# Expert and shared biases of a mixture-of-experts layer: from dense gates and a matmul to adding gathers and GpSimd

## The reference

```
k, v = xn @ key_w.T, xn @ value_w.T ; r = sigmoid(xn @ recep_w.T)
out  = x + (r * wkv_scan(decay, first, k, v)) @ out_w.T          # attention-like mixing over time
logits = xn @ gate_w.T + gate_b ; top 2 of 8 experts, weights g  # routing
y  = sum over the 2 chosen e of g_e * ((silu(xn@w1_e.T+b1_e) * (xn@w3_e.T+b3_e)) @ w2_e.T + b2_e)
z  = (silu(xn@ws1.T+bs1) * (xn@ws3.T+bs3)) @ ws2.T + bs2         # shared expert, 512 wide
out += y + z
```

## Time and profile before

| | |
|---|---|
| time, median of 3 runs | 473.65 us (469.54 to 474.90) |
| the profiled execution | 470.54 us, of which the span of the records is 468.8 us |
| PE busy | 445.1 us (95%) |
| DVE busy | 365.1 us (78%) |
| ACT busy | 239.8 us (51%) |
| POOL busy | 232.5 us (50%) |
| mean granted clock of PE | 0.981 |

### The profile page before, as it was taken

The page is one execution under the profiler, slowest core; times in us unless marked ns, Lnnn a source line. Parts: engine busy times, 40 slices in busy tenths (PEclk is TensorE's granted clock), DMA queues, the critical chain, the costliest instruction groups (busy, mean ns, idle before and its releaser), DMA issues.

```text
span 468.8 us, 8342 instructions
## 1 busy us (share of the span) xinstructions
PE 445.1 (95%) x2549; PEld 374.1 (80%) x2549; DVE 365.1 (78%) x680; ACT 239.8 (51%) x394; POOL 232.5 (50%) x224
## 2 busy tenths in 40 slices
PE   5898977979999999999998999999999999999997
PEld 4453746858888888888887879798888889898987
DVE  5968868798776987878675689996968687877863
ACT  4778735677768586876754532423324142324031
POOL 3234777354858658589744477661523425160000
PEclk9899769999999999999999999999999999999999
DMA  8999743255674854344454863726152433431001
GB/s 245 396 351 285 211 115 94 66 199 203 237 264 120 273 183 139 125 136 135 119 198 158 290 238 113 251 68 228 50 185 86 155 122 123 157 119 63 25 24 45
DMA packets 45874, 77.24 MB, mean 165 GB/s; under 512 B 5924, under 2 KB 32268, under 8 KB 45836
## 3 DMA queue, kind: packets, MB, share of 16 engines
q1 hardware_dynamic: 36924, 55.83, 33.8%
q0 software_dynamic: 8240, 20.88, 16.9%
q10 hardware_dynamic: 672, 0.04, 0.1%
HBM read 48.52 MB, written 28.21 MB: 164 GB/s over the span
## 4 chain that ended last, share of the span: by engine, by line
PE 46%; POOL 18%; issue 13%; DVE 10%; DMA 4%; ACT 4%; SPq 3%; POOLq 0%; DVEq 0%; ACTq 0%
POOL xg L1005 8%; PE ps_w L1540 5%; PE ps_w L1542 5%; PE ps_w L1541 5%; PE ps_w L1605 5%; PE ps_w L1606 5%; PE ps_w L1607 5%; PE ps_g L1082 4%; DMA w_lo<-w_all 3%; POOL den L1017 2%; PE ps_y L1082 2%; SPq L424 2%; POOL den L1016 2%; DVE stats L687 2%; POOL firsts L1024 2%
## 5 line engine op out<-in xcount | busy, mean ns | idle before, releaser
L1005 POOL DMA_INDIRECT xg<-xn_rows,tile_tok x71 | 71.4, 1006 | 21.9 <-issue 19.1
L1516 POOL DMA_INDIRECT yg<-expert_rows,rows x64 | 66.8, 1044 | 23.6 <-issue 17.1
L1082 PE MATMUL ps_g<-w_hi,x_hi 128*128 x142 | 56.7, 399 | 1.6 <-DVE x_lo L1237 1.6
L1082 PE MATMUL ps_g<-w_lo,x_hi 128*128 x142 | 56.7, 399 | 0.0
L1082 PE MATMUL ps_g<-w_hi,x_lo 128*128 x142 | 56.3, 397 | 0.0
L1647 ACT ACTIVATE sact<-ps_w,vec_b 128x512 f32<-128x512 f32 x32 | 22.0, 687 | 58.7 <-PE ps_w L1542 58.7
L1540 PE MATMUL ps_w<-col_hi,s_hi 128*128 128x512 f32 x128 | 50.5, 395 | 0.4 <-DVE shid L1758 0.4
L1542 PE MATMUL ps_w<-col_hi,s_lo 128*128 128x512 f32 x128 | 50.2, 392 | 0.0
L1541 PE MATMUL ps_w<-col_lo,s_hi 128*128 128x512 f32 x128 | 50.1, 392 | 0.0
L1082 PE MATMUL ps_y<-w_hi,h_hi 128*128 x142 | 43.1, 304 | 1.3 <-DVE h_lo L1253 1.3
L1246 DVE TENSOR_TENSOR hid<-ps_g,act 128x512 f32<-128x512 f32 (+1 forms) x36 | 23.7, 657 | 25.5 <-ACT act L1158 25.5
(11 more groups left out here) (247 smaller groups left out, 1278.5 us busy)
## 6 DMA issues: line engine op xcount, KB each, us to landing
expert_rows<-y SPq DMA_DIRECT2D x35, 256.0 KB, 2.2
w_lo<-w_all SPq DMA_DIRECT2D x16, 384.0 KB, 10.1
table<-mix_tables SPq DMA_DIRECT2D x8, 768.0 KB, 6.7
xT<-x SPq DMA_DIRECT2D x16, 256.0 KB, 6.1
xn_rows<-xn SPq DMA_DIRECT2D x16, 256.0 KB, 9.2
xn_columns<-xT SPq DMA_DIRECT2D x8, 512.0 KB
col<-xn_columns SPq DMA_DIRECT2D x8, 512.0 KB, 5.0
res<-x SPq DMA_DIRECT2D x16, 256.0 KB, 2.9
```

The costliest lines, as they stand in the source:

```text
L1005: pool.indirect_dma_start(out=xg[b][:, t, :], out_offset=None, in_=xn_d[:, :], in_offset=bass.IndirectOffsetOnAxis(ap=tile_tok[:, first_ti ...
L1082: mm = nc.tensor.matmul(out, x[:, k, :], w[:, ds(e, 1), k, cols].rearrange("p o n -> p (o n)"), start=(k == 0 and n == 0), stop=(last and ...
L1516: pool.indirect_dma_start(out=yg[a.buf(2)][:, k, q, :], out_offset=None, in_=y_d[:, :], in_offset=bass.IndirectOffsetOnAxis(ap=picked[a.bu ...
```

## The change

The bias terms leave the matmul. `b_all` becomes a table of 9 rows: `bs2`, then `b2` of the experts in falling order. In `choose` the rank of each chosen expert (8 minus its number) is kept in `rank` rather than overwritten, and clipped to 1..8 it is the row number of that expert's bias (`bias_row`, in one tile `picks` with `slots`). In the mixing stage GpSimd's gather of step a is followed by `add_biases`: once the 8 gathers have landed, 8 more indirect DMAs fetch the bias rows and add them onto `yg`; and by `add_shared`: one GpSimd addition of `bs2` onto `res`. `dense`, `terms`, `gT`, `g_now`, `rows_b`, `low_rows`, PE's 8 transposes and its 32 bias matmuls go, with their loads and waits. DVE's first 6 weight cuts (`split_lo`) stand together at the end of routing, where there were 2. DVE's first group of each step now waits for `b_bias` and `b_rows`.

```diff
-            nc.gpsimd.memset(terms[:], 0.0).then_inc(s_terms, 1)
-            pool.wait_ge(s_terms, 1)
-            nc.gpsimd.memset(terms[:, :, 3 * E:3 * E + 2], 1.0).then_inc(s_terms, 1)
...
-                own.link(nc.vector.tensor_reduce(red[:, t], work2[:, t], AX_X, ALU.max))
+                own.link(nc.vector.tensor_reduce(rank[:, 0, t], work2[:, t], AX_X, ALU.max))
...
-        MADE, BOTH, HIGH, LOW = 4, 6, 13, 2
+        MADE, BOTH, HIGH, LOW = 4, 6, 13, 6
...
-            own.link(nc.vector.tensor_copy(tile_exp[:], exp_f[:]))
-            scaled()
-            dve.wait_ge(s_terms, 2)
-            nc.vector.tensor_tensor(dense[:], score, mask[:].rearrange("p e j -> p j e"), ALU.mult).then_inc(s_terms, 1)
+            nc.vector.tensor_copy(tile_exp[:], exp_f[:]).then_inc(s_ready, 1)
+            own.link(nc.vector.reciprocal(gates[:, 0, :], red[:]))
             dve.wait_ge(s_gate, 1)
             nc.vector.tensor_tensor(gates[:, 1, :], gates[:, 1, :], gates[:, 0, :], ALU.mult)
-            dve.wait_ge(s_terms, 4)
-            nc.vector.tensor_tensor(terms[:, :, E:2 * E], dense[:], terms[:, :, 0:E], ALU.subtract
-                                    ).then_inc(s_terms, 1)
+            nc.vector.tensor_scalar(bias_row, rank[:], 1.0, float(E), ALU.max, ALU.min).then_inc(s_ready, 1)
...
-            pe.wait_ge(s_terms, 5)
-            for i in range(NSTEP):
-                mm = nc.tensor.transpose(ps_y[i // 4][:].rearrange("p t c -> p (t c)")[:, i % 4 * P:(i % 4 + 1) * P],
-                                         terms[:, i * Q:(i + 1) * Q, :].rearrange("p q n -> p (q n)"), ident[:])
-                if i % 4 == 3:
-                    mm.then_inc(c_turn, 1)
+            pe.wait_ge(s_ready, 1)
...
-            def pick(a):
-                at_least(pool, b_o, a.i * Q - Q)
-                nc.gpsimd.tensor_copy(g_now[a.buf(2)][:], gT[:, ds(a.i, 1), :].rearrange("p o n -> p (o n)")
-                                      ).then_inc(b_gc, 1)
+            def add_biases(a):
+                pool.wait_ge(b_gath[a.buf(2)], (a.uses(2) + 1) * 16 * TOPK * Q)
+                pool.sem_inc(b_go, 1)
+                for k in range(TOPK):
+                    for q in range(Q):
+                        pool.indirect_dma_start(
+                            out=yg[a.buf(2)][:, k, q, :], out_offset=None, in_=b_all,
+                            in_offset=bass.IndirectOffsetOnAxis(ap=picked[a.buf(2)][:, TOPK + k, q:q + 1], axis=0),
+                            compute_op=ALU.add
+                        ).then_inc(b_rows[a.buf(2)], 16)
+
+            def add_shared(a):
+                pool.wait_ge(b_res[a.buf(2)], (a.uses(2) + 1) * 32)
+                nc.gpsimd.tensor_tensor(res[a.buf(2)][:], res[a.buf(2)][:],
+                                        shared_b[:, None, :].broadcast_to([P, Q, C]), ALU.add).then_inc(b_bias, 1)
+
+            def prepare(a):
+                gather(a)
+                add_biases(a)
+                add_shared(a)
 
             def step(a, first, left):
-                pick(a)
                 if left > 0:
-                    gather(a.plus(1))
+                    prepare(a.plus(1))
...
-                    nc.tensor.matmul(ps_w[q][:, 0:C], g_now[a.buf(2)][:], rows_b[:, q, :],
-                                     start=True, stop=False)
                     for k in range(KC):
                         three_rows(ps_w[q][:, 0:C], a_hi, a_lo, k, slice(q * P, (q + 1) * P), o_hi, o_lo,
-                                   False, False)
+                                   k == 0, False)
...
                 if g == 0:
-                    dve.wait_ge(b_res[buf], (a.uses(2) + 1) * 32)
-                    dve.wait_ge(b_gath[buf], (a.uses(2) + 1) * 16 * TOPK * Q)
+                    dve.wait_ge(b_bias, a.i + 1)
+                    dve.wait_ge(b_rows[buf], (a.uses(2) + 1) * 16 * TOPK * Q)
...
-        "b_all": np.concatenate([get("L0_ffn_b2")] * 3 + [get("L0_ffn_bs2")[None]] * 2, axis=0),
+        "b_all": np.concatenate([get("L0_ffn_bs2")[None], get("L0_ffn_b2")[::-1]], axis=0),
```

More of the change, by code:

```diff
@@ L55 @@
 EPS = 1e-5
-TERMS = 32
 PIECE = 256
@@ L224, in _, with route @@
                 mix_vector(dve)
-def route(nc, kept, x, first, decay, vec_tf, vec_td, gate_w, gate_b, w_all, w_first, nw_d, xn_d, xT_d, ident, slots, gates,
-          tile_tok, tile_exp, w_hi, w_lo, terms, lane_i, row_of1, minus):
+def route(nc, kept, x, first, decay, vec_tf, vec_td, gate_w, gate_b, w_all, w_first, nw_d, xn_d, xT_d, ident, slots, bias_row, gates,
+          tile_tok, tile_exp, w_hi, w_lo, lane_i, row_of1, minus):
     with ExitStack() as ctx:
@@ L568, in scalar @@
                 split(i)
[L569 to L572, removed]
             for i in range(4, BOTH):
@@ L984, in sync @@
                     sp.dma_start(*loads[a - A_LOADS]).then_inc(c_ld, 16)
-                if a == A_ROWS:
-                    sp.wait_ge(c_zero, 1)
-                    for q in range(Q):
-                        sp.dma_start(rows[TERMS * q:TERMS * q + 3 * E + 2, q, :], b_all).then_inc(c_rows, 16)
                 if a == 4 * LAST_V + 1:
@@ L1194, in scalar @@
             cut_x(0)
-            for h in range(2):
-                act.wait_ge(c_turn, h + 1)
-                nc.scalar.activation(gT[:, 4 * h:4 * h + 4, :].rearrange("p j n -> p (j n)"),
-                                     ps_y[h][:].rearrange("p t c -> p (t c)"), ACT.Copy).then_inc(c_gT, 1)
             silu(0)
@@ L1217, in scalar @@
                     halves(v)
-                if a == A_HI:
-                    act.wait_ge(c_rows, 16 * Q)
-                    act.wait_ge(c_zero, 1)
-                    nc.scalar.activation(rows_hi[:], rows[:], ACT.Copy).then_inc(c_rhi, 1)
                 if a == DUOS - 4:
@@ L1365, in vector, with mix @@
                     differences(v + 1)
-                if a == A_ZERO + 2:
-                    low_mask()
-        return sync, gpsimd, tensor, scalar, vector, (c_y, c_yc, c_wlo, c_gT, c_rowsb)
-def mix(nc, kept, over, x, xT_d, y_d, y_stored, coef_stored, tab_d, out, slots, gates, vr_hi, vr_lo, raw_s13, raw_o, raw_s2,
-        col0, col_hi0, col_lo0, vec_b1, vec_b3, gT, rows_b):
+        return sync, gpsimd, tensor, scalar, vector, (c_y, c_yc, c_wlo, (c_ld, len(loads)), s_ready)
+def mix(nc, kept, over, x, xT_d, y_d, y_stored, coef_stored, tab_d, out, picks, b_all, shared_b, gates, vr_hi, vr_lo, raw_s13, raw_o,
+        raw_s2, xT, x_hi, x_lo, vec_b1, vec_b3):
     with ExitStack() as ctx:
@@ L1388, in mix @@
         splits = ((raw_s13, s13_hi, s13_lo), (raw_o, o_hi, o_lo), (raw_s2, s2_hi, s2_lo))
-        xT = [col0, sb("col1", [P, KC, STEP], F32)]
-        x_hi = [col_hi0, sb("col_hi1", [P, KC, STEP], F32R)]
-        x_lo = [col_lo0, sb("col_lo1", [P, KC, STEP], F32R)]
         res = [sb(f"res{b}", [P, Q, C], F32) for b in range(2)]
         yg = [sb(f"yg{b}", [P, TOPK, Q, C], F32) for b in range(2)]
-        picked = [sb(f"rows{b}", [P, TOPK, Q], I32) for b in range(2)]
+        picked = [sb(f"rows{b}", [P, 2 * TOPK, Q], I32) for b in range(2)]
         sa = sb("sa", [P, KC * B, TIMES + 1], F32)
-        g_now = [sb(f"g_now{b}", [P, P], F32R) for b in range(2)]
         table = [sb(f"table{b}", [P, 3, KC, TIMES], F32) for b in range(2)]
@@ L1424, in mix @@
         b_xlo = sem("b_xlo")
-        b_gc = sem("b_gc")
+        b_rows = [sem(f"b_rows{b}") for b in range(2)]
+        b_bias = sem("b_bias")
         b_v = sem("b_v")
```

95 lines of the change are left out of this document (27 added, 68 removed).

## The result

The changed kernel takes **545.12 us** (median of 4 runs, 543.77 to 545.86) against 471.6 us on the same chip: 1.155 times as long, 95% interval 1.146 to 1.164. The forecast was 512 us with a range up to 537. The direction and the mechanism came true; the time lies above the range. The profiled execution took 543.77 us, its span is 542.0.

What follows compares the result with a forecast made beforehand. GpSimd was taken to bound mixing: first `prepare` ends at 292.7, seven more at 28.7 us reach 493.6, plus 17 us tail and 1.7 us beyond the span give 512 us; range 494 to 531, widened to 490 to 537.

Steps and rivals of the forecast that it cites:

- the mechanism: Mixing stage: GpSimd becomes the bound at 26 to 31 us a step, where PE would need 25.0; chance 0.81.
- A: GpSimd's price for one adding gather of bias rows in `prepare`: taken as 1.24 us, between 0.95 and 1.53.
- The rule weighed beside it: GpSimd computes one descriptor pair per DMA operation regardless of bytes, so the whole 0.58 us would belong to the addition.
- signs of being wrong: GpSimd still waits for `b_slot`; median A outside 0.95 to 1.53 us; DVE waits for landing well after GpSimd's addition.
- The sum: GpSimd's work for one mixing step: 11.9 + 1.85 + 0.3 + 12.0 + 2.4 + 0.2 = 28.7 us.
- The upper end: Mixing stage: adding costs GpSimd all of the difference, A = 1.53 us, a step 31.0 us, the kernel 531 us.
- The second rival: Mixing stage: adding is dearer still, 1.79 us each as routing's mean, a step 33.1 us, 547 us; chance 0.11.
- The head: Start of mixing: second `prepare` ends at 321.4 where its rows were wanted at 298.90, most of the loss.
- The tail: From the last `prepare`, ending at 493.6, to the span's end: 17 us, against 18.7 before, PE having worked ahead.
- The gain taken off beforehand: Mixing stage: removing PE's 32 bias matmuls saves 3.8 us, 0.48 us a step, only while PE sets the pace.

Runs made afterwards that it cites:

- the run with three lengths: Changed kernel with each step's bias gathers replaced by six: rows of 1 KB, 512 B and 2 KB, each with and without addition; 508.40 us, one run.

## Why the prediction was wrong, point by point

- **Right: the mechanism.** GpSimd bounds the mixing stage, with no wait for DVE left in its loop; DVE stands at the first group of `experts`, and PE waits for `shid` behind it. Without the adding gathers the loss is zero, so they carry it. The addition of `bs2` costs something too, some 3.7 us by one pair of traces, which the products that went make up for in part.
- **The step that failed: "I take half for the addition, A = 1.24 us, because it is equally near to both rows."** It measured 1.54 us, and 1.70 in the mean. The half was no reading of the trace: two causes lay between two rows, and one of them was worth nothing. The rule weighed beside it gave all of the 0.58 us to the addition, and the run with three lengths bears it out (0.6 us, at every length).
- **Two of the prediction's own signs of being wrong came up.** The median of A is 1.540 us, just outside 0.95 to 1.53. And in four of the eight steps the landing of the added rows, not the addition of `bs2`, ends DVE's wait, 0.7 to 4.9 us after that addition is done. In the step shown above the addition ends at 422.20 + 2.93 = 425.13, and the use comes 4.9 us later:
```profile
430.03 0.88 DVE L1662 SCALAR_TENSOR_TENSOR res<-yg,gates,res 128x256 f32<-128x256 f32 x2 [11.30 <-DMA yg<-b_all,rows]
```
  The sum had no term for that landing (4.4 us in the median, up to 8.7). It moves single uses, but not the pace, since GpSimd goes on without waiting for them.
- **The upper end was no bound.** 531 us took 1.53, the least price of the earlier trace rows, although the mean of the earlier trace rows was 1.79. Above the least price lies what DVE does in SBUF beside it, 0.16 us in the mean, as the two kernels with added DVE work bear out. The second rival came nearest (547 us), but for its number only: it named weight loads, and I gave it 0.11. My range ended at 537.
- **The rest of the sum holds.** With 1.70 in place of 1.24 the eight gathers take 8 x 1.70 + 2.1 = 15.7 us. The first `prepare` then ends at 261.7 + 34.7 = 296.4 (measured: the use at 296.45), a step takes 32.4 us (measured 32.34), and the last use comes at 522.9 (measured 522.84). That these agree so closely is in part luck, since smaller terms were off both ways: the landing wait is 2.6 us, not 2.15; the eight take 15.9, not 15.7; and the addition of `bs2` adds 1.8 to a step, not 2.6. Its record is 2.93 us long, not 2.41, but it begins 0.55 us before the record of the last adding gather ends; behind plain gathers it took 2.41 and did not overlap.
- **The head:** 22.5 us forecast, 29.9 measured, by the same price counted twice.
- **The tail:** 17 us forecast, 19.2 measured. I had PE fast and ahead there. In fact its last wait, 5.30 us, left it at a granted clock of 0.50 for 12 matmuls, an estimated 2.5 us. The second rival's text mentioned the clock, but said it costs only where PE's work no longer fits in GpSimd's step, and the sum left it out of the tail.
- **The gain taken off beforehand** (3.8 us for PE's products): 2.6 us by one trace, and in the kernel that still adds `bs2` on GpSimd nothing at all, since that addition holds DVE up.

## What to carry to other kernels

A price between two rows that differ in two ways isn't halved: either a row must part the causes, or the range takes the dearer end with its mean, not its minimum. Work that moves to an engine with 50% idle time must be summed per step against the step of the bounding engine, with landing waits in between; here eight small DMAs added 16 us to a step that had 13 us free. And before a cost is moved off the bounding engine, its worth is measured by leaving it out altogether: here that would have shown 0.3%.

## What the runs showed of the hardware that was not expected

- A gather of 128 rows takes at the least 1.53 us on GpSimd with addition and 0.95 without, for rows of 512 B, 1 KB or 2 KB alike, and with addition for distant rows as well as for eight near ones. With addition every row is a packet of its own, without it four rows of 1 KB share one.
- DVE instructions in SBUF stretch such a gather, some not at all and others by up to 1 us (2.58 the longest in the changed kernel; 2.93 with the one-input instructions added), with two inputs and with one fast input. DVE instructions with one input from PSUM don't. It works the other way too: GpSimd's 2.42 us addition made a 1.22 us DVE instruction take 3.33.
- A DMA with addition from SBUF to SBUF, 512 pieces of 1 KB, takes 1.96 us on GpSimd and lands 7.2 us after its issue.
- What stays open: why the addition costs GpSimd 0.6 us, whether the packets have to do with it, and whether it goes by the number of rows. Every adding gather here had 128.
